# Rotary cross-attention of the second layer: first stacks copied without the trip through memory, two input loads moved up, first expert loads held until the last stack is in place

## What is computed

```
# second layer, attention: q from x, k and v from the context, both rotated
q = x @ Wq + bq
kv = context @ Wkv + bkv
k, v = jnp.split(kv, 2, axis=-1)
...
q = _larope(q, Lq)
k = _larope(k, Lk)
scores = jnp.einsum('bhqd,bhkd->bhqk', q, k) * SCALE
scores = jnp.where(context_mask[:, None, None, :], scores, -jnp.inf)
attn = jax.nn.softmax(scores, axis=-1)
out = jnp.einsum('bhqk,bhkd->bhqd', attn, v)
...
# second layer, experts: each row goes to the expert of its largest probability
h = jax.nn.relu(jnp.einsum('bsd,edf->besf', x, W1) + b1[:, None, :])
y = jnp.einsum('besf,efd->besd', h, W2) + b2[:, None, :]
out = jnp.einsum('bse,besd->bsd', gates, y)
```

## Time and profile before

| | us |
|---|---|
| median of 3 runs | 1340.39 (1337.57 to 1344.4) |
| the profiled execution | 1344.11 |
| its span | 1342.4 |
| second layer's attention, from its first DMA issue to beat 0's first scores_T | 871.7 to 942.1 |
| its beats 0 to 7 and tail, to the first expert tile on TensorE | 942.1 to 1151.6 |
| experts of the second layer, rest | 1151.6 to 1342.4 |

### The profile page before, as it was taken

How to read it: one execution, slowest core, us unless ns; L and a number is a source line. 1 busy time by engine, 2 the same in 40 slices (tenths; PEclk the granted TensorE clock), 3 DMA queues, 4 the chain that set the end, 5 groups by cost and what they waited for, 6 DMA issues and landing times. The chain is left out here.

```text
span 1342.4 us, 27195 instructions
## 1 busy us (share of the span) xinstructions
PE 1171.6 (87%) x8287; PEld 944.8 (70%) x8333; DVE 796.2 (59%) x3047; ACT 624.2 (47%) x1515; POOL 540.8 (40%) x866
## 2 busy tenths in 40 slices
PE   4689999999987999899999999446988877699996
PEld 3466667666654888789999999433656644689995
DVE  4588878888873388865333343176868965423231
ACT  2278787878885233143333333111655544233331
POOL 3334454545433254545333333231544533333331
PEclk9799999999999999899999999866999988799998
DMA  4766675545421971122222222167634884511110
GB/s 107 172 139 167 140 168 112 113 101 115 97 38 20 379 203 33 48 41 37 41 34 40 41 33 36 17 148 167 152 84 116 167 272 152 189 34 48 39 37 5
DMA packets 113526, 136.98 MB, mean 102 GB/s; under 512 B 23115, under 2 KB 99801, under 8 KB 108476
## 3 DMA queue, kind: packets, MB, share of 16 engines
q1 hardware_dynamic: 98152, 106.08, 33.1%
q0 software_dynamic: 15232, 29.17, 9.6%
HBM read 101.85 MB, written 35.97 MB: 103 GB/s over the span
## 5 line engine op out<-in xcount | busy, mean ns | idle before, releaser
L797 DVE CUSTOM_DVE_ANT_0 att_masked_scores<-att_S,Bm 128x256 bf16<-128x256 f32 x512 | 190.3, 418 | 38.2 <-PE att_S L539 26.9
L2459 ACT ACTIVATE moe_hT<-moe_H,moe_b 128x128 f32<-128x128 f32 x312 | 89.0, 368 | 171.5 <-PE moe_H L2372 171.0
L672 ACT ACTIVATE att_PT<-att_T 128x512 f32<-128x512 f32 x256 | 146.2, 591 | 47.6 <-PE att_T L561 43.6
L2384 PE MATMUL moe_Z<-moe_W,moe_hT 128*128 x624 | 141.6, 380 | 0.8 <-DVE moe_z L2684 0.8
L2384 PEld LDWEIGHTS moe_Z<-moe_W,moe_hT 128*128 128x128 f32 x624 | 115.5, 190 | 15.5 <-issue 1.2
L2547 POOL DMA_INDIRECT x<-Y,X x39 | 63.6, 1632 | 154.7 <-DVE Y L2695 150.8
L539 PE MATMUL att_S<-L_KS,L_QS 96*128 96x256 bf16 x512 | 99.3, 276 | 20.3 <-DMA L_KS<-att_k_dram 13.8
L561 PE MATMUL att_T<-L_QS,L_KS 99*128 99x256 bf16 x512 | 97.4, 272 | 11.2 <-ACT att_T L677 3.7
L1825 DVE TENSOR_REDUCE out_mx<-out_S 128x2 f32<-128x512 f32 x128 | 85.4, 685 | 34.5 <-PE out_S L1257 33.4
L2684 DVE TENSOR_TENSOR moe_z<-moe_Z,moe_b 128x256 f32<-128x256 f32 x39 | 16.6, 424 | 141.9 <-PE moe_Z L2384 141.9
L2372 PEld LDWEIGHTS moe_H<-moe_aT,ff_w 128*128 128x128 f32 x832 | 96.8, 192 | 3.1 <-issue 1.9
(11 more groups left out here) (469 smaller groups left out, 2524.2 us busy)
## 6 DMA issues: line engine op xcount, KB each, us to landing
moe_W<-in_L_ffn_W SPq DMA_DIRECT2D x16, 1024.0 KB, 13.7
L_W<-in_L_ffn_W POOLq DMA_DIRECT2D x12, 1024.0 KB, 10.5
att_q_dram<-att_pq SPq DMA_DIRECT2D x16, 384.0 KB, 4.4
att_k_dram<-att_pk SPq DMA_DIRECT2D x16, 384.0 KB, 2.8
L_QS<-att_q_dram SPq DMA_DIRECT2D x16, 384.0 KB, 4.9
L_KS<-att_k_dram SPq DMA_DIRECT2D x16, 384.0 KB, 8.1
L_QS<-att_q_dram SPq DMA_DIRECT2D x16, 256.0 KB, 5.7
L_KS<-att_k_dram SPq DMA_DIRECT2D x16, 256.0 KB, 8.7
```

What stands on the lines that cost most here:

```text
L672: nc.scalar.activation(PT[:, h % 8, :], bankT[h % 2][:, :], ACT.Exp).then_inc(exp_done, 1)
L797: ins = nc.vector.tensor_tensor_reduce(masked_scores[:, h % 2, u, :], bankS[h % 2][:, u * SEQ:(u + 1) * SEQ], masks[m // B][0][:, u * SEQ: ...
L2384: ins = nc.tensor.matmul(bankZ[:, 0:D], eT[:, s % 2, f * P:(f + 1) * P], w2e[:, f, :], start=(f == 0), stop=(f == NF - 1))
L2459: ins = nc.scalar.activation(eT[:, s % 2, g * P:(g + 1) * P], bankH[half][:, f * P:(f + 1) * P], ACT.Relu, bias=b1[:, bass.ds(e * NF + g, 1)])
```

## The change

- **First stacks (sequence 0).** `first_stack` copies each finished part straight from pq or pk into the stack, as soon as that part is done: per side 12 DMAs of 64 KB, each from 128 partitions (512 bytes each) into 8 partitions. They replace one write and three reads per side. The key row stays.
- **Two pq and two pk**, so parts of sequence m no longer wait for the write of m-1; `parts_free` waits for m-2.
- **Loads moved up on SP**: context and x of sequence 2, the value weights, x of 3 and 4 and context 3 are all issued ahead of the first stacks.
- **Order**: `turn_rows(2)` goes ahead of all scores on TensorE, `queries(2)` behind the 16 heads of sequence 0, `project_values` of 1 and 2 move to head 14 of beats 0 and 1. READY's root of sequence 3 is made by GpSimd between parts of sequence 2. `spread_parts` of 1 go both ahead of `stack` of 1.
- **Experts**: GpSimd issues experts 0 to 3 together in beat 5, behind a wait for both stacks of sequence 7 (`last_stack`).

The core of the diff:

```
-FILL = ("k", 0), ("x", 0), ("k", 2)
+FILL = ("k", 0), ("x", 0), ("k", 2), ("x", 2)
-LAST_FILL = {2: (("x", 2),), 5: (("q", 2),), 9: (("m", 0),), 10: (("v", 0),), 12: (("x", 3),), 13: (("v", 1),), 15: (("v", 2),)}
+LAST_FILL = {7: (("m", 0), ("q", 2)), 10: (("v", 0),), 12: (("x", 3),)}
+LATE_VALUES = {(0, 14): (("v", 1),), (1, 14): (("v", 2),)}
...
+            def first_stack(side):
+                parts, dst, at = ((pq[0], QS, q_place), (pk[0], KS, k_place))[side]
+                for done, s in ((part1, at[0]), (part2, at[1]), (part3, at[2])):
+                    sp.wait_ge(done[side], 1)
+                    for row, q_run, k_run in STACKS:
+                        a, b = (q_run, k_run)[side]
+                        if a <= s < b:
+                            for cc in range(NC):
+                                first = row + (s - a) * DK + cc * (DK // NC)
+                                sp.dma_start(dst[first:first + DK // NC, at_place(0), :, :], parts[:, s, cc, :]).then_inc(stacked[side][0], 16)
+                if side:
+                    key_row(0)
...
-            spread_parts(0, 1)
-            spread_parts(0, 0)
             load_context_of(sp, mem, 2)
             load_sums(2)
-            stack(0, 1)
-            stack(0, 0)
             load_values(sp, mem)
-            spread_parts(1, 1)
-            stack(1, 1)
-            spread_parts(1, 0)
-            stack(1, 0)
             load_sums(3)
-            spread_parts(2, 1)
-            stack(2, 1)
             load_sums(4)
             load_context_of(sp, mem, 3)
+            sp.wait_ge(mem["rows_in"], 32)
+            first_stack(1)
+            first_stack(0)
+            spread_parts(1, 1)
+            spread_parts(1, 0)
+            stack(1, 1)
+            stack(1, 0)
+            spread_parts(2, 1)
             max_to_queries(0)
+            stack(2, 1)
             spread_parts(2, 0)
             stack(2, 0)
...
+            def last_stack():
+                for side in range(2):
+                    pool.wait_ge(*in_place(M - 1, side))
...
-                if b == 4:
+                if b == 5:
+                    last_stack()
                     first_expert()
-                if b == 5:
                     second_expert()
                     third_and_fourth_expert()
```

More of the change, by code:

```diff
@@ L912, in rotary_tasks @@
     last = {"o": QUADS * B, "t": EARLY_SEQUENCES1 - 1, "l": EARLY_SEQUENCES1 - 1, "n": EARLY_SEQUENCES1 - 1}
-    return more + tuple((k, n) for k, n in units if 0 <= n < last.get(k, B))
+    return more + tuple((k, n) for k, n in units if 0 <= n < last.get(k, B)) + LATE_VALUES.get((b, h), ())
 ROUTE_TASKS = {1: (("l", -3),), 5: (("n", -3),), 13: (("t", -2),)}
@@ L951, in rotary_memory @@
             "tk": part("W2", 2, 0),
-            "pq": three(half["W2", 2][:, 2 * NC * SEQ:2 * NC * SEQ + PARTS]), "pk": three(half["W2", 3][:, 0:PARTS]),
+            "pq": [three(half["W2", 2][:, 2 * NC * SEQ:2 * NC * SEQ + PARTS]), three(half["W1", 3][:, 0:PARTS])],
+            "pk": [three(half["W2", 3][:, 0:PARTS]), three(half["W1", 3][:, PARTS:2 * PARTS])],
             "QS": stacks(W1[:, 4:7, :].rearrange("p e n -> p (e n)").bitcast(BF16)),
@@ L1102, in stack, with key_row @@
                 if side:
-                    sp.dma_start(KS[ROW_KEY:ROW_KEY + 1, at_place(m), :, :],
-                                 mem["key_off"][m:m + 1, :].unsqueeze(1).broadcast_to([1, H, SEQ])).then_inc(stacked[1][p], 16)
+                    key_row(m)
+            def key_row(m):
+                sp.dma_start(KS[ROW_KEY:ROW_KEY + 1, at_place(m), :, :],
+                             mem["key_off"][m:m + 1, :].unsqueeze(1).broadcast_to([1, H, SEQ])).then_inc(stacked[1][m % 3], 16)
+            def first_stack(side):
[10 more added lines that the diff above has]
+                    key_row(0)
             def spread_parts(m, side):
-                parts, dst = ((pq, q_dram), (pk, k_dram))[side]
+                parts, dst = ((pq[m % 2], q_dram), (pk[m % 2], k_dram))[side]
                 sp.wait_ge(part3[side], m + 1)
-                if m >= 2:
-                    sp.wait_ge(stacked[side][(m - 2) % 3], 16 * N_STACK[side] * ((m - 2) // 3 + 1))
+                if m >= 3:
+                    sp.wait_ge(*in_place(m - 2, side))
                 sp.dma_start(dst[m % 2].rearrange("s (c r) t -> r s c t", r=P), parts[:, :, :, :]).then_inc(spread[side], 16)
@@ L1409, in _ @@
             keys(2)
+            turn_rows(2)
             for h in range(H // 2):
@@ L1413, in _ @@
                 scores(*scores_of(-1, h))
-                if h == 2:
-                    turn_rows(2)
-                if h == 5:
+                if h == 7:
+                    turn_max(0)
                     queries(2)
-                if h == 9:
-                    turn_max(0)
                 if h == 10:
@@ L1423, in _ @@
                     turn_rows(3)
-                if h == 13:
-                    project_values(1)
-                if h == 15:
-                    project_values(2)
             early = lambda n: 0 <= n < EARLY_ONES - 1
@@ L1454, in _ @@
                         turn_out(turning)
+                    if h == 14 and b < 2:
+                        project_values(b + 1)
                     if h == 1 and early(b - 3):
@@ L1512, in first_part @@
             def first_part(m, side):
-                f, parts, at = ((fq, pq, q_place), (fk, pk, k_place))[side]
+                f, parts, at = ((fq, pq[m % 2], q_place), (fk, pk[m % 2], k_place))[side]
                 act.wait_ge(f_sum[side], m + 1)
-                if m >= 1:
-                    act.wait_ge(spread[side], 16 * m)
+                if m >= 2:
+                    act.wait_ge(*parts_free(m, side))
                 nc.scalar.activation(flat(parts[:, at[0], :, :]), f[:, :], ACT.Copy).then_inc(part1[side], 1)
             def second_part(m, side):
-                r, parts, at = ((rq, pq, q_place), (rk, pk, k_place))[side]
+                r, parts, at = ((rq, pq[m % 2], q_place), (rk, pk[m % 2], k_place))[side]
                 act.wait_ge(rest1[side], m + 1)
@@ L1619, in _ @@
                         bring_rows(b + 4)
+                    if h == 14 and b < 2:
+                        value_rows(b + 1)
                     quad = QUADS * b + (h - 5) // 4
@@ L1657, in rest @@
             def rest(m, side):
-                f, r, parts, at = ((fq, rq, pq, q_place), (fk, rk, pk, k_place))[side]
+                f, r, parts, at = ((fq, rq, pq[m % 2], q_place), (fk, rk, pk[m % 2], k_place))[side]
                 pool.wait_ge(part1[side], m + 1)
@@ L1743, in _ @@
                 for side in (1, 0):
+                    if (m, side) == (READY - 1, 0):
+                        input_roots(READY)
                     rest(m, side)
```

28 lines of the change are left out of this document (12 added, 16 removed).

## The result

| | median, us | lowest to highest | runs |
|---|---|---|---|
| before | 1340.0 | 1337.6 to 1344.4 | 8 |
| after | 1333.3 | 1330.3 to 1337.2 | 8 |

The ratio is 0.9944, 95% interval 0.9928 to 0.9961: 6.7 us faster. The forecast was 1330 and a range of 1323 to 1344.

A forecast was written before the change was run, and what follows sets the result against it. TensorE was taken as full in the beats, VectorE close behind, with holes before beat 0 and in beat 5. Gains of 2.3 (7.7 - 3.4 - 2.0) and 7.65 us off the 1340.4 median gave 1330.4, forecast 1330, range 1323 to 1344.

The forecast's parts named there:

- the sum of 9.95 us: Whole kernel: forecast gain, 2.3 us net from the filling part plus 7.65 from the last stack.
- The start of the first scores: Filling part: direct copies let TensorE's first scores start at 904.0 in place of 908.2.
- I take 0.65 us per copy: First stacks: assumed SyncE cost of each of 24 small copies, putting their end at 902.0.
- Rival 1: First stacks: copies bound at the receiving partitions, 1.3 us each, 15.6 us more before first scores; 1346 us; chance 0.25.
- From first scores to beat 0: Filling part: unbroken heads and later products bring beat 0's first scores_T near 934.4 against 942.1, 7.7 us earlier.
- the norm of input 3, its turn, the wide bias and moments of input 4 about 3.2 together: End of the filling part: these pieces add 3.2 us after sequence 1's eight heads and project_values(0).
- What is paid back: Beats 0 and 1: moved project_values cost 3.4 us, beat 0's first products at low clock 2.0.
- The last stack: Beat 5: without expert 0 sequence 7's reads go out in one row; 5.65 of 7.35 us stall go, 1.7 stay.
- the 7.65 us: Beat 5: gain from the last stack, 5.65 us of stall and 2.0 of lost clock.
- I cost this at nothing: Behind the last stack: experts 0 to 3, 8.4 MB, take 25 us to about 1103, before the first expert tile at 1151.55.
- Rival 3: Beats 6 and 7: held expert loads delay the maxima rows; 3 us late would give 1333 us; chance 0.10.
- Rival 2: Beat 5: sequence 7's key row takes 13.1 us again, 6.0 of the stall stay; 1337 us; chance 0.20.

The follow-up runs named there:

- e3: After, with sequence 0's stacks written to memory and read back in place of the 24 direct copies; ratio to before 0.9940.
- e2: Before, with only the expert loads changed: experts 0 to 3 all wait for sequence 7's stack in beat 5; ratio to before 0.9965.
- e4: After, with project_values of sequences 1 and 2 back in the filling part (heads 13 and 15); ratio to before 0.9934.
- e1: After, with the expert loads as before: expert 0 in beat 4, experts 1 to 3 in beat 5, no wait for the last stack; ratio to before 0.9980.
- e12: e10 with experts 2 and 3 loaded in beat 6, only 0 and 1 in beat 5; ratio to before 0.9919, median 1333.0 us.
- e5: After unchanged, timed again beside other experiments and before; ratio to before 0.9943.
- e10: e7 with SyncE's sequence 6 rows and last two experts' loads held until the first expert tile's gather has landed; ratio to before 0.9923.
- e11: After, with 8 of the q side's 12 direct copies issued on ScalarE's queue in place of SyncE's; ratio to before 0.9922.
- e9: After, with SyncE's sequence 6 rows and last two experts' loads held until the first expert tile's gather has landed; ratio to before 0.9938.
- e6: e3 with the loads of wo and bo issued earlier, after sequence 1's stacks in place of sequence 2's; ratio to before 0.9929.
- e7: e6 with project_values of sequences 1 and 2 in the filling part, as in the kernel before; ratio to before 0.9931.
- e8: After, with expert 0 loaded in beat 4 again and experts 1 to 3 still held for the last stack; ratio to before 0.9976.

## Why the prediction came out right, and where it was not

The total was right: 1330 forecast against 1333.3, the sum of 9.95 us against 6.7 and 7.8 by the medians. Several steps were not.

- **The start of the first scores: wrong by 2.7 us.** Forecast 904.0 on before's clock; measured 904.72 + 2.0 = 906.7. The copies began at 887.0 for 886.4 (0.6 late). They went out one every 0.68 us, so "I take 0.65 us per copy" was nearly right; but the sum 24 x 0.65 left out the key row that stands between them (0.6), and with the 0.03 too little for each copy the 25 issues took 17.05 us for 15.6. From the last issue to the scores it took 2.7 us for 2. Of the 4.2 us meant to be gained by direct copies nothing is left: e3 starts earlier without them, and e2, with the old order as well, starts at 34.5 on the stage clock. The 908.2 that the step started from was itself at the late end of a scatter of 2 us. Rival 1, 1.3 us a copy, did not occur, and neither did the 1.2 us estimated from the Trainium skill (SBUF — State Buffer, "Door 1: The DMA port swizzle"): 64 KB passed every 0.64 us on one queue and every 0.58 on two.
- **From first scores to beat 0: wrong the other way.** Forecast 30.4 us, measured 26.9. The step "the norm of input 3, its turn, the wide bias and moments of input 4 about 3.2 together" and the eight heads were added up as if one followed the other; with input 3's norm ready early they run side by side: 8.2 us from the end of the rotation to beat 0 in place of 12.3. The two errors cancel, which is why beat 0 at 934 looked right (933.6 on before's clock): luck. The gain of the filling part is the order's, not the copies'.
- **What is paid back: right in cause and nearly in size.** Beats 0 and 1 grew by 4.6 us (47.3 against 42.7) for the 3.4 + 2.0 counted, with `queries(3)` at 3.50 us for the low clock, 1.6 more than at full clock. Both terms go with the values: e4, which has them in the filling part, has beats 0 and 1 at 42.7 as in before, and `queries(3)` at full clock:

```profile
939.44 1.89 PE L1241 MATMUL out_A<-out_xT,L_W 128*128 128x256 f32 x8
```

But I had not asked what the values cost where they stood, 2.1 to 2.7 us and 0.9 to 1.0 more in beat 2; so moving them was neutral.
- **The last stack: mechanism right, the 7.65 us too many.** The stack goes out in one row, the clock stays at 1.00 to the end of beat 5 (1082.3), and beat 5 is 7.0 us shorter. The key row took 10.1 us, not 8.8, so 2.49 us of stall stayed, not 1.7. The runs give the hold 4.7 us (e2, interval 2.2 to 7.3). Two terms failed. Part of beat 5's gain was not the hold's: e1, without it, has beat 5 2.1 us shorter than before. And "I cost this at nothing" left out what comes behind: beats 6 and 7 took 34.6 us in e1 and 35.5 to 36.4 in the kernels that hold all four experts and copy directly. That the 8.4 MB behind the stack make it is near at hand, but no run shows it. e12 halves them, waits only 0.4 us for the maxima rows, and still takes 36.1. What differs as well is the clock at the start of beat 6, 0.86 in after and 1.00 in e1:

```profile
1082.00:1092.00 10.00, 8.44 (x80) 5.54 (x79) 7.86 (x26) 5.38 (x11) 5.51 (x17) 0.86 1.04 404
```
```profile
1090.00:1100.00 10.00, 8.28 (x86) 5.27 (x83) 8.82 (x31) 6.13 (x14) 4.53 (x16) 1.00 0.51 177
```

So part of the low clock was not removed but moved from beat 5 into beat 6.
- **Rival 3 was real, if small:** TensorE waited 0.6 us for the maxima rows in after, 1.2 in e5 and 2.5 in e10, against 0.3 in before. Rival 2 (13.1 us) did not occur; 10.1 lies between it and the 8.8 of the forecast.
- **Not foreseen:** the first expert tile's gather, 3 us shorter in after. With the 2.0 of the first layer it makes the profiles differ by 13.8 us; the profile of before lay 4.1 above its median, that of after 3.0 below.

## What to carry to other kernels

Measure each landmark from a common point of the same program before adding up terms: two wrong terms of about 3 us gave a right sum here, and only taking the pieces apart showed that the piece with the most code, the direct copies, gained nothing that can be measured. Look for the small product or norm whose input comes late before shortening the long chain beside it. A load that is held back frees the place where it stood, and something of that is paid in the next place (here 1.0 to 1.9 us of 5.0), so time both places. Take each landmark at the same instruction in every kernel, and compare an unchanged kernel with itself, before a difference of 1 or 2 us between two profiles is believed.

## What the runs showed of the hardware

- Small copies from 128 partitions into 8, 64 KB in pieces of 512 bytes, went out one every 0.68 us on one queue (0.61 us of it the issue) and the DMA engines kept up at 103 GB/s (after); issued from two queues at once they moved at 113 GB/s (e11), and from first issue to first use 24 of them took 19.8 and 20.0 us.
- Two writes of 384 KB to memory and six reads of 128 to 384 KB brought the same stacks no later than these 24 direct copies (first scores at 33.5 to 35.4 in five profiles against 35.0 to 37.1 in seven), though the bytes move twice.
- A gather of 128 rows reached TensorE 4.1 to 4.2 us after its issue with the traffic behind it held (e9, e10, e12). With 4.5 MB of other loads, the first of them issued 0.1 to 0.9 us behind it, it took 5.7 to 6.8 (before, e2, e3, e6, e7), and with them 1.2 to 1.5 us behind 4.1 to 4.9 (after, e1, e4, e5, e8, e11).
